# Slices sums rows before it multiplies, and four smaller moves: L2Project's third parts to GpSimd, router rows and weights to SyncE, L1's residual beside its products

## The reference, cut to what matters

```python
# L1 graph block (end): h = relu(batchnorm((x + agg) @ W1)) @ W2, then two norms over all rows, relu
x = x + relu(graphnorm(h))            # x inside the block is layernorm(x) again: x + ln(x) + out
# L1 feed-forward: every row goes to one of 32 experts (argmax of x @ router_w.T)
# L2 feed-forward: every row goes to the 2 best of 16 experts
# L2 graph block: proj_s = f @ W_s.T, proj_t = f @ W_t.T, kept as sums of three bf16 parts
# L3 feed-forward, B = 1, 8 heads, 64 slices, 64 columns a head:
fx_mid = x @ W_fx + b_fx
slice_weights = softmax(((x @ W_x + b_x) @ W_slice + b_slice) / temp)   # over the 64 slices
slice_norm = slice_weights.sum(over rows)
slice_token = einsum(fx_mid, slice_weights) / (slice_norm + 1e-5)
# attention between the 64 tokens of a head, then back to the rows by slice_weights, @ W_out
```

## Time and profile before

| | us |
|---|---|
| median of 3 runs | 5455.45 (5451.37 to 5457.28) |
| profiled execution | 5460.66 |
| its span | 5458.8 |
| PE, PEld busy | 4354.3 (80%), 2868.9 (53%) |
| DVE, ACT busy | 3479.1 (64%), 2303.0 (42%) |
| POOL busy | 3320.4 (61%) |

### The profile page before, as it was taken

The page is one execution under the profiler, slowest core; times in us unless marked ns, Lnnn a source line. Parts: engine busy times, 40 slices in busy tenths (PEclk is TensorE's granted clock), DMA queues, the critical chain, the costliest instruction groups (busy, mean ns, idle before and its releaser), DMA issues. The chain is left out here.

```text
span 5458.8 us, 88501 instructions
## 1 busy us (share of the span) xinstructions
PE 4354.3 (80%) x20192; PEld 2868.9 (53%) x20192; DVE 3479.1 (64%) x12190; ACT 2303.0 (42%) x7944; POOL 3320.4 (61%) x3594
## 2 busy tenths in 40 slices
PE   6978777999957777656799968888696688878768
PEld 4533436899823335443455547666594333346536
DVE  8977884411167774545555558887415688878875
ACT  6910552333333334123555545554143455545421
POOL 7777775666467774451577757775124477758710
PEclk8966998999956667677999989999697899999978
DMA  2443336698667773152444458886474488877500
GB/s 69 156 144 104 105 105 204 240 301 290 200 178 206 207 208 73 56 129 78 125 131 129 129 156 287 277 277 186 147 210 123 135 230 232 232 208 230 174 19 24
DMA packets 528344, 916.64 MB, mean 168 GB/s; under 512 B 95861, under 2 KB 378436, under 8 KB 519396
## 3 DMA queue, kind: packets, MB, share of 16 engines
q0 software_dynamic: 154432, 449.76, 29.5%
q1 hardware_dynamic: 330254, 346.48, 20.2%
q10 hardware_dynamic: 43158, 114.74, 6.7%
HBM read 741.02 MB, written 169.60 MB: 167 GB/s over the span
## 5 line engine op out<-in xcount | busy, mean ns | idle before, releaser
L1212 PE MATMUL bank<-small 128*125 128x256 f32 x1660 | 737.3, 557 | 281.6 <-DVE small L1175 169.9
L1156 POOL DMA_INDIRECT small<-tabA,idxD x830 | 800.7, 965 | 263.9 <-issue 150.2
L1212 PEld LDWEIGHTS bank<-small 128*125 128x125 f32 x1660 | 339.5, 252 | 674.0 <-DVE small L1175 372.4
L2649 POOL DMA_INDIRECT big<-tabT,edge x415 | 403.9, 973 | 246.4 <-SPq L200 120.3
L3185 POOL DMA_INDIRECT small<-tabC,idxD x415 | 409.5, 987 | 185.6 <-SPq L200 59.4
L2923 POOL DMA_INDIRECT big<-tabB,idxD x415 | 399.2, 962 | 169.1 <-issue 89.6
L1066 POOL DMA_INDIRECT eaS<-edge,rowE x391 | 393.2, 1006 | 163.5 <-issue 115.2
L1762 DVE COPY small<-bank 128x256 f32<-128x256 f32 x176 | 74.7, 424 | 617.9 <-PE bank L1819 601.3
L1187 DVE TENSOR_TENSOR big<-big,bank 125x256 f32 x830 | 345.5, 416 | 148.1 <-PE bank L1212 131.7
L3263 PE MATMUL bank<-big,cst 128*125 128x512 f32 x830 | 424.7, 593 | 0.7 <-ACT big L3250 0.7
L1717 POOL DMA_INDIRECT small<-tabA,small x176 | 168.0, 955 | 380.8 <-PE bank L1795 186.8
(11 more groups left out here) (531 smaller groups left out, 10802.2 us busy)
## 6 DMA issues: line engine op xcount, KB each, us to landing
big<-in_L_w ACTq DMA_DIRECT2D x56, 1024.0 KB
small<-eaS SPq DMA_DIRECT2D x415, 128.0 KB
eaS<-small SPq DMA_DIRECT2D x415, 128.0 KB, 3.5
big<-eaS SPq DMA_DIRECT2D x415, 128.0 KB, 3.5
edge<-in_ea SPq DMA_DIRECT2D x390, 128.0 KB
big<-in_L2f_w ACTq DMA_DIRECT2D x64, 512.0 KB
big<-rowsD SPq DMA_DIRECT2D x104, 256.0 KB, 4.2
ytab<-small SPq DMA_DIRECT2D x120, 128.0 KB
```

Of the source, the lines that this page charges most:

```text
L1156: g.indirect_dma_start(out=self.gb[k % self.RG], out_offset=None, in_=K.tabA, in_offset=row_index(K.idxD, k)).then_inc(*self.got.up(k))
L1212: p.matmul(self.K.bank[k % 4][0:PT, 0:D], self.oh[k % self.RO][:, 0:PT], self.gb[k % self.RG], start=True, stop=True).then_inc(*self.summe ...
L2649: g.indirect_dma_start(out=self.rows(k)[:, 0, :], out_offset=None, in_=K.tabT, in_offset=row_index(K.idxS, k)).then_inc(*self.got.up(k))
```

## The change

Each edit is one of placement or of order; only Slices computes in another order.

- **L1Mlp.** The layer norm of x and its addition to x go from the last loop into the first, between the four `bn_stats` of the tile. The last loop adds the bank alone, takes the statistics of the tile before, and has four banks. The final Relu, two instructions of 3125 columns, becomes five pairs of 625, and TensorE starts behind the first pair. GpSimd's part is as it was.
- **Routers of L1 and L2.** Rows are stored by SyncE, a tile in two pieces, and the second weights of the experts are issued earlier: L1's in L1Mlp, L2's at the start of L2Out.
- **L2Project.** The cast to the third part is GpSimd's.
- **Slices, start.** The weights are loaded and multiplied into each other (`fold`) beside L3Elu.
- **Slices, loop and middle.** The products with W_fx go out of the loop. TensorE adds up `xn^T @ weights`, two products of 512 columns a tile, in banks 4 and 5; GpSimd adds up the weights themselves. After the last tile the sums are multiplied with W_fx, 24 products of 64 columns, and the bias with the summed weights; the norm is made by a product with ones, and its reciprocal has 512 columns.

```diff
@@ Moe
-            self.store_row(a, i)
+            store_rows(s, K.tabA[t * PT:(t + 1) * PT, :], self.xn[t % self.RN][0:PT, :], self.x_out.up(t))
...
@@ L1Mlp.tensor
-        p.wait_ge(*self.final.n(1))
         for t in range(T):
-            if t >= 2:
-                p.wait_ge(*self.out.n(t - 1))
+            if t % 5 == 0:
+                p.wait_ge(*self.final.n(t // 5 + 1))
+            if t >= 4:
+                p.wait_ge(*self.out.n(t - 3))
@@ L1Mlp.vector, first loop
+                if f == 1:
+                    ln_apply(K, v, t, self.tmp[t % 2][0:PT, :]).then_inc(*self.normed.up)
+                if f == 3:
+                    v.wait_ge(*self.normed.n(t + 1))
+                    v.tensor_tensor(K.xt(t), K.xt(t), self.tmp[t % 2][0:PT, :], ALU.add).then_inc(*self.joined.up)
+                    v.wait_ge(*self.joined.n(t + 1))
...
@@ L2Project.gpsimd
         for t in range(T):
-            if t:
-                g.wait_ge(*self.product.n(t))
-            self.source.gpsimd(g, 3)
+            for m in range(2):
+                g.wait_ge(*self.less[1].n(2 * t + m + 1))
+                g.tensor_copy(self.third(t, m, 2), self.rest(t, m)).then_inc(*self.part[2].up)
@@ L2Project.scalar
-            for c, late in ((2, 6), (1, 5), (0, 4)):
+            for c, late in ((1, 5), (0, 4)):
@@ Slices.gpsimd
+        for t in range(T):
+            g.wait_ge(*self.soft.n(t + 1))
+            sv = self.sw[0:PT, t * 512:(t + 1) * 512]
...
+                g.tensor_tensor(w, w, sv, ALU.add).then_inc(*self.weighed.up)
@@ Slices.tensor, loop
-                for q in range(4):
-                    m = p.matmul(K.bank[4 + q][:, 0:129], self.sw[0:PT, t * 512 + q * 128:t * 512 + (q + 1) * 128],
-                                 self.fx[t % 4][0:PT, q * 129:(q + 1) * 129], start=(t == 0), stop=(t == T - 1))
+                for c in range(2):
+                    m = p.matmul(K.bank[4 + c][:, :], self.xn[t % self.RX][0:PT, c * 128:(c + 1) * 128],
+                                 self.sw[0:PT, t * 512:(t + 1) * 512], start=(t == 0), stop=(t == T - 1))
...
-                for c in range(2):
-                    m = p.matmul(K.bank[3][0:PT, :], xT[:, c, :], self.wf[:, c * 512:(c + 1) * 512], start=(c == 0), stop=(c == 1))
-                m.then_inc(*self.values.up)
@@ Slices.tensor, middle
+        p.matmul(K.bank[6][0:64, :], K.ones[0:PT, 0:64], self.weight[0:PT, :], start=True, stop=True).then_inc(*self.norm.up)
...
+        for h in range(8):
+            at = slice(h * 64, (h + 1) * 64)
+            p.matmul(K.bank[0][0:64, at], self.bf[0:PT, at], self.weight[0:PT, at], start=True, stop=False)
+            for c in range(2):
+                m = p.matmul(K.bank[0][0:64, at], self.wf[:, c * 512 + h * 64:c * 512 + h * 64 + 64], self.sums[c][:, at], start=False, stop=(c == 1))
@@ order of the stages (SyncE, TensorE)
+            l3_ffn.fold(p)
+            s.wait_ge(*l1_mlp.flipped.all)
+            m1.weights_sync(s, 0)
+            s.wait_ge(*l1_mlp.second.all)
+            m1.weights_sync(s, 1)
...
+            for i in range(m2.n_w):
+                m2.weights_sync(s, i)
```

More of the change, by code:

```diff
@@ L1295, in __init__ @@
         self.logits = K.mark(T)
-        self.x_out = K.ring(self.RN, T)
+        self.x_out = K.ring(self.RN, T, parts=1 if shared else 2)
         if not shared:
@@ L1364, in scores_sync, with weights_sync @@
             s.wait_ge(*self.normed.n(t + 1))
[L1365 to L1371, removed]
+            store_rows(s, K.tabA[t * PT:(t + 1) * PT, :], self.xn[t % self.RN][0:PT, :], self.x_out.up(t))
+        for t in range(T - self.RN, T):
+            s.wait_ge(*self.x_out.n(t))
+    def weights_sync(self, s, i):
+        lo, hi = i * self.step, min((i + 1) * self.step, self.E)
+        s.dma_start(self.w2s[:, lo * self.w2:hi * self.w2].rearrange("p (e c) -> p e c", c=self.w2),
+                    self.K.a[self.key + "w"].rearrange("p (e c) -> p e c", c=self.ecols)[:, lo:hi, self.w2off:]).then_inc(*self.weights.up)
     def scores_gpsimd(self, g):
@@ L2245, in scalar @@
         a.wait_ge(*self.scale2.n(1))
-        for o in range(2):
-            ins = a.activation(self.h2v[:, o, :], self.h2v[:, o, :], ACT.Relu, scale=self.q[2][:, o:o + 1], bias=self.q[3][:, o:o + 1])
-        ins.then_inc(*self.final.up)
+        for c in range(5):
+            at = slice(c * 5 * PT, (c + 1) * 5 * PT)
+            for o in range(2):
+                ins = a.activation(self.h2v[:, o, at], self.h2v[:, o, at], ACT.Relu, scale=self.q[2][:, o:o + 1], bias=self.q[3][:, o:o + 1])
+            ins.then_inc(*self.final.up)
     def vector(self, v):
@@ L2317, in vector @@
         for t in range(T):
[L2318 to L2322, removed]
-            v.wait_ge(*self.back.n(t + 1))
-            v.tensor_tensor(K.xt(t), K.xt(t), K.bank[t % 2][0:PT, 0:D], ALU.add).then_inc(*self.out.up)
-            v.wait_ge(*self.out.n(t + 1))
-            ln_tile(K, v, t, K.xt(t))
+            v.wait_ge(*self.back.n(t + 1))
+            v.tensor_tensor(K.xt(t), K.xt(t), K.bank[t % 4][0:PT, 0:D], ALU.add).then_inc(*self.out.up)
+            if t >= 1:
+                v.wait_ge(*self.out.n(t))
+                ln_tile(K, v, t - 1, K.xt(t - 1))
+        v.wait_ge(*self.out.all)
+        ln_tile(K, v, T - 1, K.xt(T - 1))
         v.wait_ge(*own.all)
@@ L3513, in __init__ @@
         self.wq, self.wk, self.wv = W(64), W(64), W(64)
+        self.weight, self.nr = W(512), W(512)
+        self.sums = [W(512) for _ in range(2)]
         self.tickets = [K.ticket() for _ in range(12)]
@@ L3546, in sync @@
             load(s, ticket, dst, a[name])
+    def sync(self, s):
+        K = self.K
         K.meet(s, "s")
@@ L3601, in tensor @@
         K.meet(p, "p")
[L3602 to L3605 removed]
+        p.wait_ge(*self.weighed.all)
+        p.matmul(K.bank[6][0:64, :], K.ones[0:PT, 0:64], self.weight[0:PT, :], start=True, stop=True).then_inc(*self.norm.up)
+        p.wait_ge(*self.kept_a.n(1))
+        p.wait_ge(*self.kept_v.n(1))
+        for h in range(8):
[3 more added lines that the diff above has]
+                m = p.matmul(K.bank[0][0:64, at], self.wf[:, c * 512 + h * 64:c * 512 + h * 64 + 64], self.sums[c][:, at], start=False, stop=(c == 1))
@@ L3692, in vector @@
         self.stats.vector(v)
-        for f in self.fx:
-            ins = v.memset(f.rearrange("p (q c) -> p q c", c=129)[:, :, 128:129], 1.0)
-        ins.then_inc(*self.one.up)
         for i in range(T + 3):
@@ L3725, in vector @@
             if i < T:
[L3726 to L3728 removed]
+                if i >= self.RX:
+                    v.wait_ge(*self.slot.n(i - self.RX + 1))
+                ln_apply(K, v, i, self.xn[i % self.RX][0:PT, :]).then_inc(*self.normed.up)
         K.meet(v, "v")
[L3730 to L3741 removed]
+        nr = self.nr[0:64, :]
+        v.tensor_copy(self.sums[1], K.bank[5][:, :]).then_inc(*self.kept_v.up)
+        v.wait_ge(*self.norm.n(1))
+        v.tensor_scalar(nr, K.bank[6][0:64, :], 1e-5, None, ALU.add).then_inc(*own.up)
+        v.wait_ge(*own.all)
+        v.reciprocal(nr, nr).then_inc(*self.inverse.up)
+        v.wait_ge(*self.inverse.n(1))
+        v.wait_ge(*self.folded_t.n(1))
+        v.tensor_tensor(self.tT[0:64, :], K.bank[0][0:64, :], nr, ALU.mult).then_inc(*self.tokens.up)
         v.wait_ge(*self.qm.n(1))
```

87 lines of the change are left out of this document (34 added, 53 removed).

## The result

The changed kernel takes 5381.41 us (median of 4 runs, 5380.94 to 5385.56), the kernel before in the same sitting 5456.36 (5451.37 to 5457.98). The ratio is 0.9866, 95% interval 0.9849 to 0.9883. The profiled execution has a span of 5383.8 us against 5458.8.

What follows compares the result with a forecast made beforehand. Five stages run one after another, each priced alone: VectorE and GpSimd in L1Mlp, store waits in low-clock routers, loads before Slices. Terms -14.8 - 6.0 - 13.0 - 2 - 21.5 - 13.7 + 3 = -68 gave median 5387.5 us, range 5368 to 5405.

Steps and rivals of the forecast that it cites:

- the likeliest case: Whole kernel: all terms as summed, 5387 us, own range 5378 to 5396, chance .62.
- L1Mlp: L1Mlp's last loop: VectorE's gain of 25 mostly cut off by GpSimd's scatters at pitch 1.26; -14.8 us.
- The tail of 0.9 in the first loop: L1Mlp's first loop gets longer by the last tile's apply and add, 0.9 us with the wait between.
- Routers: Routers of L1 and L2: waits for late row stores go once the weights move out; -6.0 and -13.0 us.
- The fear that the 8 MB would reach into L2's router: L2's router: weights at 227 GB/s last five microseconds into it; if waits keep their share, -8 instead of -13.
- L2Project: L2Project: turn falls from 3.96 to 3.85, each GpSimd cast costing VectorE 0.25; -2 us.
- Rival B: L2Project: the lock costs a whole GpSimd operation each time, turn 4.57, +12 instead of -2; total 5402, chance .15.
- Slices, start and loop: Slices: loads and products beside L3's ELU stage, -21.5 us; loop turn from 4.86 to 4.37 and first tile, -13.7 us.
- Slices, middle: Between Slices loop and tokens: added products, +3 us taken; +4.1 at low clock, -0.3 at high, bound by the reciprocal.
- Rival C: Nothing blocks in L2Project (-12 for -2) and a router runs partly at 2.4 GHz; total 5370 to 5377, chance .15.
- Rival D: Routers: PE's waits are VectorE's own lateness, not the stores', so routers give nothing; total 5406, chance .05.
- Rival E: Slices loop: TensorE stays at 1.2 GHz, about 7.7 us a tile, +83; total 5470, chance .02.

Runs made afterwards that it cites:

- experiment 5: Changed kernel with the second expert weights issued by SyncE inside the routers again, stores still by SyncE in two pieces; ratio to the kernel before 0.9876.
- experiment 7: Changed kernel with expert weights inside the routers again and rows stored by ScalarE in two pieces; ratio to the kernel before 0.9875.
- experiment 8: Changed kernel with expert weights inside the routers again and rows stored by SyncE in one piece; ratio to the kernel before 0.9907.
- experiment 2: Changed kernel with 13 of GpSimd's 25 scatters moved from L1Mlp's last loop to L1's router; ratio to the kernel before 0.9836.
- experiment 4: Changed kernel with 13 scatters moved to L1's router and L2Project's casts behind the dot product; 5366.48 us, ratio to the kernel before 0.9813.
- experiment 6: Changed kernel, weights still early, but rows stored by ScalarE in one piece as before; ratio to the kernel before 0.9859.
- experiment 3: Changed kernel with GpSimd's two L2Project casts also waiting for VectorE's dot product; ratio to the kernel before 0.9844.
- experiment 9: Changed kernel with GpSimd's addition of softmax weights in the Slices loop waiting for ScalarE's Exp; ratio to the kernel before 0.9874.
- experiment 1: The changed kernel run and profiled once more, no edit; ratio to the kernel before 0.9867.

## Why the prediction was right, point by point

The forecast was 5387.5 and the measured median is 5381.4. It was the likeliest case: six of the seven steps went the way they were given, as large as forecast, within 0.5 us, or larger, and the seventh, the middle of Slices, cost next to nothing. None missed by over 5 us. The seven stretches gave -79.4 where the sum had -68, and 4.3 came back in the others. So the total came nearer than the sum of its parts, and that is luck: 11.4 us of misses, nearly all to one side, were cut by 4.3 us of which no term had spoken.

- **L1Mlp, -18.0 for -14.8.** That GpSimd would cut VectorE's gain off was the step that mattered; without it the term would have been -25. Three sizes were off. The stage passes its meeting when GpSimd's queue gets there, not when its last scatter is through: scatters started until 2265.9, and the next stage ran from 2263.5. Counted from the stage's start, the last scatter itself was through at 148.8, where the sum had 148.7; the 3.3 us between are the miss. The tail of 0.9 in the first loop did not appear; in its place a scatter waited 2.20 for an earlier one's landing while the second transfer of L1's weights, issued at 2219.3, was under way. The three kernels without these weights in L1Mlp (experiments 5, 7 and 8) have 0.3 of that wait and took 144.1 to 144.9 for the stage, the others with its full scatters and the moved norm 145.2 to 146.5: the early weights cost about 1 us there, a price that the forecast did not have. And VectorE alone would have gained more than 25: its tile took 0.86 and not the 1.02 that was left over, and with GpSimd out of the way the stage lost 28.6 and 29.5 us (experiments 2 and 4).
- **Routers, -7.4 for -6.0 and -15.7 for -13.0.** The waits at L274 were the right thing to count. PE's one remaining wait is 2.6 and 1.9, where 3.1 was kept. The fear that the 8 MB would reach into L2's router did not come true: DMA share there is 0.33. They moved at 366 GB/s from 3753.4 to 3777.0, where the forecast took 227, and were in 8 us before the router began. That the weights' traffic makes the stores late was right, by experiment 6; what the forecast did not see is that stores in two pieces alone would have given 10 of the 16 us in L2's router. The text also took the ring of rows for two; it has six, so a store can be late by several tiles before L274 waits for it.
- **L2Project, -4.4 for -2.** 0.20 a cast was measured where 0.25 was taken. Rival B, a whole GpSimd operation each time, is out for this kernel: 19 turns of 4.57 did not come. The Trainium skill's rule of an exclusive lock ("SBUF — State Buffer", "Who interferes with whom") is right in that these two meet, but not in that one stands still for the whole of the other: in the turn shown, casts and second subtractions would need 0.80 + 0.76 = 1.56 one after the other (the two pairs by themselves in experiment 3) and took 1.34 together (2544.82 to 2546.16). The earlier trace rows pointed there already: 0.93 at most, where 0.40 and 0.61 one after the other are 1.01. The prediction's estimate of 0.38 for a cast, by its page "GPSIMD Engine Reference", agrees with the shortest, 0.39 to 0.40; the median without a subtraction beside it is 0.45.
- **Slices, start and loop, -21.0 and -13.2, for -21.5 and -13.7.** As worked out. The addition of GpSimd, 1.27, lies exactly where it was put, beside L3737 and L3739, and experiment 9 shows what the cover is worth: 5.8 us where the text had 10.
- **Slices, middle, +0.3 for +3.** The mis-sized term: the forecast priced all products at the low level, the trace shows them at the high one (1.98 for the last pair, granted clock 1.00). The other end, bound by the reciprocal at about 4.0, was the right one; it took 3.35. In seven of the eleven later profiles the middle took 12.0 to 12.2, +1.8 to +2.0. In these seven and in no other the granted clock of the 11 us before the tokens is 0.84 and not 1.00, by one stretch of 3.4 us at 0.50. In experiment 1's profile it falls on the last pair, which takes what the forecast had for it (3.5), and the products behind it are at the high level again:

```profile
5301.23 3.55 PE L3601 MATMUL bank<-big,small 125*128 125x512 f32 x4 [2.40 <-DVE big L3729]
```

PE had stood for 2.4 before this pair in either profile, so why the clock fell in one and not in the other stays open.
- **Rivals C, D, E.** The routers did not leave 0.50. The stores did land earlier. The Slices loop stayed at 0.97.

Still open: the experts of L1 lost 3.6 us. Their length runs from 210.5 to 216.1 over the eleven profiles with no order that I can tie to an edit, but like the stretch up to L1Mlp none falls below the one profile of before (210.2).

## What to carry to other kernels

When one engine's work is taken out of a loop, look for the engine that was merely keeping pace: GpSimd issued one scatter a tile at 1.26, hidden behind 1.9 of VectorE, and became the end of the stage at once. In these loops work given to GpSimd was free where VectorE had one SBUF operand or none; where it had two, VectorE paid 0.27 for 0.41 us beside an addition, and 0.20 a subtraction beside casts. So gate such work by the right neighbour, not by its input. Move heavy loads away from a stage that waits for its stores; where they must stay, a row store of 125 partitions should go in pieces of 112 and 13.

## What the runs showed of the hardware that was not expected

Beside the weights' transfers, stores of 125 rows in one piece made L2's router 10.4 us longer than the same stores in two (SyncE: 53.8 and 43.4), although both move the same bytes; without other traffic it made no difference (35.6 and 35.6, here ScalarE's single pieces against SyncE's pairs). A GpSimd cast and a VectorE subtraction that meet slow each other, 0.45 to 0.53 and 0.42 to 0.615.
